# Attention loops written out, ordered first loads, and v projected in one run

## The reference, cut to what matters

```
h = layernorm(x)
q, k, v = split(h @ w_qkv + b_qkv)            # 16 heads of 16 features
attn = softmax(q @ k.T * 16**-0.5, axis=-1)   # per head, 4096 x 4096
x = x + layernorm((attn @ v) @ w_proj + b_proj)
x = x + layernorm(ffn(layernorm(x)))
```

## Time and profile before

| | before |
|---|---|
| median of 3 runs | 3265.24 us |
| profiled execution: time | 3264.68 us |
| profiled execution: span of the trace | 3262.9 us |
| mean granted TensorE clock | 0.967 |
| TensorE / DVE / ScalarE / GpSimd busy | 95 / 87 / 77 / 8% |

### The profile page before, as it was taken

The page is one execution under the profiler, slowest core; times in us unless marked ns, Lnnn a source line. Parts: engine busy times, 40 slices in busy tenths (PEclk is TensorE's granted clock), DMA queues, the critical chain, the costliest instruction groups (busy, mean ns, idle before and its releaser), DMA issues.

```text
span 3262.9 us, 80910 instructions
## 1 busy us (share of the span) xinstructions
PE 3107.3 (95%) x26983; PEld 1366.9 (42%) x26983; DVE 2833.9 (87%) x3108; ACT 2504.8 (77%) x4551; POOL 260.8 (8%) x810
## 2 busy tenths in 40 slices
PE   8799999999999999999999999999999999988883
PEld 3444443344344434443444344434434444456652
DVE  5389999999999999999999999999999999456666
ACT  6158888888888888888888888888888888733333
POOL 2300000000000000000000000000000000011103
PEclk9689999999999999999999999999999999989996
DMA  7700101010101011000101010101010100000001
GB/s 259 88 1 1 34 8 28 14 27 14 25 17 24 18 21 21 21 21 15 27 14 27 12 30 11 30 8 34 8 34 8 34 9 22 1 1 0 0 0 52
DMA packets 27390, 83.30 MB, mean 26 GB/s; under 512 B 4641, under 2 KB 15633, under 8 KB 24018
## 3 DMA queue, kind: packets, MB, share of 16 engines
q1 hardware_dynamic: 26818, 77.84, 10.7%
q0 software_dynamic: 272, 1.05, 0.1%
HBM read 57.90 MB, written 20.97 MB: 24 GB/s over the span
## 4 chain that ended last, share of the span: by engine, by line
PE 93%; DVE 2%; issue 2%; ACT 1%; DMA 1%; POOL 1%; DVEq 0%; SPq 0%; POOLq 0%; ACTq 0%
PE ps L1022 41%; PE ps L1031 36%; PE ps L1239 3%; PE ps L998 3%; PE ps L1188 2%; PE ps L957 2%; PE ps L1041 1%; PE ps L1228 1%; PE ps L971 1%; PE ps L1163 1%; PE ps L1049 1%; PE ps L949 1%; DMA q_stack<-qk_parts 1%; ACT q_raw L619 0%; PE ps L1205 0%
## 5 line engine op out<-in xcount | busy, mean ns | idle before, releaser
L750 DVE TENSOR_REDUCE partial<-ps 128x1 f32<-128x1024 f32 x2048 | 2482.1, 1223 | 179.1 <-PE ps L998 156.0
L569 ACT ACTIVATE work<-ps 128x512 f32<-128x512 f32 x4096 | 2203.3, 597 | 366.3 <-PE ps L1022 151.3
L998 PE MATMUL ps<-k_stack,q_stack 48*128 48x512 f32 x4096 | 1523.2, 451 | 25.2 <-DMA q_stack<-qk_parts 17.0
L1022 PE MATMUL ps<-q_stack,k_stack 64*128 64x512 f32 x4096 | 1513.1, 449 | 21.0 <-issue 19.4
L1031 PE MATMUL ps<-work,v_head 128*32 128x256 f32 x16384 | 1300.9, 392 | 0.0
L1022 PEld LDWEIGHTS ps<-q_stack,k_stack 64*128 64x128 f32 x4096 | 634.8, 185 | 822.2 <-ACT work L569 695.3
L998 PEld LDWEIGHTS ps<-k_stack,q_stack 48*128 48x128 f32 x4096 | 635.4, 187 | 60.9 <-DVE partial L750 32.8
L1031 PEld LDWEIGHTS ps<-work,v_head 128*32 128x32 f32 x16384 | 330.3, 108 | 701.3 <-ACT work L569 575.5
L415 POOL CAST nm_parts<-negmax 128x4 bf16<-128x4 f32 x128 | 24.8, 193 | 2267.5 <-DVE negmax L757 2266.6
L1239 PE MATMUL ps<-k_raw,q_raw 128*128 128x256 f32 x512 | 127.3, 405 | 17.8 <-ACT q_raw L619 17.8
L619 ACT ACTIVATE q_raw<-ps 128x1024 f32<-128x1024 f32 x32 | 32.7, 1023 | 131.5 <-PE ps L1228 131.5
(11 more groups left out here) (128 smaller groups left out, 1110.9 us busy)
## 6 DMA issues: line engine op xcount, KB each, us to landing
k_stack<-qk_parts SPq DMA_DIRECT2D x96, 256.0 KB, 4.2
q_stack<-qk_parts SPq DMA_DIRECT2D x96, 256.0 KB, 4.1
qk_parts<-qk_part SPq DMA_DIRECT2D x32, 512.0 KB, 2.8
x_sb<-L_attn_x SPq DMA_DIRECT2D x8, 512.0 KB, 10.9
out<-work SPq DMA_DIRECT2D x8, 512.0 KB, 2.9
k_raw<-L_ffn_aux_values SPq DMA_DIRECT2D x1, 1024.0 KB
work<-L_attn_w_qkv POOLq DMA_DIRECT2D x1, 768.0 KB, 7.7
q_raw<-L_ffn_aux_keys SPq DMA_DIRECT2D x1, 512.0 KB
```

Of the source, the lines that this page charges most:

```text
L569: act.activation(probs[:, g % DEPTH, a, :], ps[:, bank, :], ACT.Exp, scale=SCALE).then_inc(exp_done, 1)
L750: dve.tensor_reduce(partial[:, k // 4, k % 4:k % 4 + 1], ps[:, 2 * slot:2 * slot + 2, :], AX.XY, ALU.max).then_inc(max_used, 1)
L998: last = pe.matmul(ps[:, 2 * slot + e, :], q_stack[HALF:HALF + ROWS, b1, c * CH + (k // 4) * P:c * CH + (k // 4 + 1) * P], k_stack[HALF:HA ...
L1022: pe.matmul(ps[:, bank, :], k_stack[0:HALF, b, P * g:P * (g + 1)], q_stack[0:HALF, b, at:at + CH], start=True, stop=True).then_inc(s_ready, 1)
```

## The change

- TensorE's loop over two heads each is replaced by Python loops: heads 0 to 14 are written out.
- ScalarE's two nested loops are replaced by one Python loop over the passes 0 to 62, with constants in all waits.
- SP waits for groups 0 and 2 of parts_out, issues the six loads of head 0 for slots 3 to 5 (semaphore first_max_in), then the six for slots 0 to 2 (first_score_in), then waits for groups 1 and 3. The loads of head 1 wait for pv_done like those of all later heads.
- TensorE projects all eight chunks of v before the maximum pass, and none between its matmuls. The maximum pass waits for first_max_in, the first score for first_score_in.

```diff
@@ sync
-            for g in range(4):
-                sp.wait_ge(parts_out[g], 16 * (NC + 1))
-
-            def load_stack(h, b, after=None):
+            def load_first(slots, done):
+                for n in slots:
+                    for stack, qk, part in ((k_stack, 1, SLOT_K[n]), (q_stack, 0, SLOT_Q[n])):
+                        sp.dma_start(stack[SLOT_ROW[n]:SLOT_ROW[n] + D, 1, 0:T].bitcast(F32),
+                                     parts_dram[qk, part, 0:D, :]).then_inc(done, 16)
+
+            def load_stack(h, b, after):
                 for n, (row, pq, pk) in enumerate(zip(SLOT_ROW, SLOT_Q, SLOT_K)):
                     for m, (stack, qk, part) in enumerate(((k_stack, 1, pk), (q_stack, 0, pq))):
-                        if after is not None:
-                            sp.wait_ge(pv_done, after + (2 * n + m) * LOAD_EVERY)
+                        sp.wait_ge(pv_done, after + (2 * n + m) * LOAD_EVERY)
                         sp.dma_start(stack[row:row + D, b, 0:T].bitcast(F32), parts_dram[qk, part, h * D:(h + 1) * D, :]
                                      ).then_inc(stack_in[b], 16)
 
-            load_stack(0, 1)
-            load_stack(1, 0)
+            for g in (0, 2, 1, 3):
+                sp.wait_ge(parts_out[g], 16 * (NC + 1))
+                if g == 2:
+                    load_first((3, 4, 5), first_max_in)
+                    load_first((0, 1, 2), first_score_in)
+            load_stack(1, 0, 1 + CREDIT[pv_done])
@@ scalar
-            def attend_head(h, b):
-                with act.Fori(0, PAIRS - 1) as j:
-                    attend(h * PAIRS + j, (b, j * 2 + 2))
-                attend(h * PAIRS + (PAIRS - 1), (1 - b, 0))
-
-            with act.Fori(0, H // NB - 1) as r:
-                attend_head(r * NB, 1)
-                attend_head(r * NB + 1, 0)
-            attend_head(H - 2, 1)
-            with act.Fori(0, PAIRS - 1) as j:
-                attend(j + (H - 1) * PAIRS, (0, j * 2 + 2))
+            for it in range(ITS - 1):
+                h, j = (it + 1) // PAIRS, (it + 1) % PAIRS
+                attend(it, ((h + 1) % NB, 2 * j))
@@ tensor
-            with pe.Fori(0, NC // 4) as c2:
+            with pe.Fori(0, NC // 2) as c2:
                 for b in range(2):
                     for j in range(2):
                         project_v(c2 * 2 + b, b, j)
@@ tensor, maximum pass
-            pe.wait_ge(stack_in[1], 16 * LOADS)
+            pe.wait_ge(first_max_in, 16 * LOADS // 2)
             for c in range(AHEAD):
                 for k in range(16):
                     for e in range(2):
                         max_half(k, e, c, 1, c, k % 2)
-                    if k % 4 == 1:
-
-                        project_v(c * 2 + (NC // 2 + k // 8), k // 8, k // 4 % 2)
             pe.wait_ge(v_evac, 2 * NC + CREDIT[v_evac])
@@ tensor, attention
             pe.wait_ge(rows_set, 2)
+            pe.wait_ge(first_score_in, 16 * LOADS // 2)
             for g in range(LAG):
                 step(g, 0, 1, 0, chunks_ahead(1, 0), None)
-            with pe.Fori(0, H // NB - 1) as r:
-                next_loaded(r * NB, 1, r + 1)
-                next_loaded(r * NB + 1, 0, r + 2)
-            next_loaded(H - 2, 1, H // NB)
+            for h in range(H - 1):
+                next_loaded(h, (h + 1) % NB, h // NB + 1)
```

More of the change, by code:

```diff
@@ L208, in sandwich_kernel @@
         stack_in = [sem(f"stack_in{b}") for b in range(NB)]
+        first_max_in = sem("first_max_in")
+        first_score_in = sem("first_score_in")
         s_ready = sem("s_ready")
```

## The result

The changed kernel takes 3212.51 us (median of six runs, 3209.84 to 3213.14) against 3265.3 us before (six runs, 3263.46 to 3269.75): a ratio of 0.9834, 95% interval 0.9821 to 0.9847, or 53 us less. The forecast was 3199.1 us, 66 less, with a range of 3191 to 3215. The time lies near the upper end of that range, and outside the 3193 to 3207 to which the forecast gave a chance of 0.77.

A forecast was written before the change was run, and what follows sets the result against it. TensorE, busy 95% of the span, was taken as the bound, time being won where it stands still or another engine paces it. 3264.7 - 35.5 (loops) - 30.1 (start) = 3199.1 us, range 3191 to 3215.

The forecast's parts named there:

- Start: Ahead of attention: v in one run, ordered loads and a denser maximum pass win 30.1 us, bounds 28.8 to 34.0.
- the low end: Maximum pass: 28.8 us won if the whole pass runs at half clock, against 30.1 forecast.
- A second HAM failure mode: psum-queue depth-cycling: Maximum pass: small idle times between matmul groups bring the clock down; by this rule the gain is 28.8, not 30.1 us.
- Loops, the size: Attention passes 1 to 62: writing the loops out cuts 2571.34 us to 2535.8, a gain of 35.5 us.
- That is my price for every pass: Attention loop: every pass takes 40.90 us, as one pass of the already written-out heads does.
- a loss of 0.1 a pass: ScalarE in attention: bound on what constant waits could cost on each of 62 passes, 6 us; 0 was taken.
- Loops, the split: Attention loop: 29.8 us from six TensorE rounds at 5.0 and 5.7 us from about 30 ScalarE back edges.
- a start-up that gains only half: Rival, ahead of attention: second half of the v run at half clock, ending 16 us later; 3215 us, chance 0.06.
- The loops are not the cause: Rival, attention: the six passes have "issue" anyway, only the start-up wins, nothing of the 29.8; 3229 us, chance 0.04.
- the stop comes back in the straight code: Rival, attention: one in ten of about 200 code packets stops TensorE 1 us, returning 20 us; 3219 us, chance 0.06.
- slower: Rival, attention: all 200 code fetches late by over 0.33 us; at 0.5 us each 3299 us; chance 0.02.
- Instruction fetch mechanics: TensorE's attention loop: fetch is mostly hidden but a taken branch outside the window waits, so all 29.8 us goes.

The follow-up runs named there:

- the run of this part alone: Changed kernel with both engines' loops back, keeping only the ordered loads and v in one run: 3237.55 us, ratio 0.9904 to the kernel before.
- the run that waits for them: Changed kernel with v cut to four chunks first and eight pieces back between maximum matmuls, loads in the new order: 3224.49 us.
- with two waits and with one: Two: the changed kernel, 3212.51 us. One: the same without ScalarE's pv_done wait ahead of a step's first exponential, 3198.77 us.
- the half pieces: Changed kernel without ScalarE's pv_done wait, five v chunks before the maximum pass, the rest as half pieces within it: 3190.16 us.

## Why the prediction was right or wrong

*Start.* Right, in size and cause: 30.1 us forecast, 29.1 in the trace, 29.5 in the run of this part alone. v's end was put at 111.7 and is 111.2 (it began 1.2 us later, at full clock from the first piece: 1.00 from 83 to 98, where the kernel before had 0.89 from 82 to 98); six loads at about 100, 100.82 in the run that waits for them. GpSimd was done with the bias at 116.9 and not at 114, which nothing waited for. Of the 38 reductions I let 9 run at full clock; the 48.55 us from the first to the 39th (111.89 to 160.44) against 47.6 fit two or three, so the low end was nearer. That the first reduction came 0.7 us earlier than forecast made up for most of it. The rule that the prediction took from the Trainium skill ("TensorE: Matmul & The Clock Gate", A second HAM failure mode: psum-queue depth-cycling) points the same way, but the page speaks of a clock that swings between its two levels; here it fell once, between 115 and 117, and stayed at 0.50 to 170.

*Loops, the size.* 35.5 us forecast, 25.5 in the trace. The step that failed is "That is my price for every pass": 40.90 us, read between 2685.76 and 2726.66. That pass has TensorE written out but ScalarE inside its loop. The state after the change, both written out, stood one pass earlier in the same trace, between these two copies:

```profile
2644.67 0.39 ACT L592 ACTIVATE o_sb<-ps 128x256 f32<-128x256 f32 x1
...
2685.76 0.39 ACT L592 ACTIVATE o_sb<-ps 128x256 f32<-128x256 f32 x1
```

It is 41.09 us. The value products around a row step show why, in this pass and then in the one of 40.90: 1.50 and 1.44 us, the same two numbers as with two waits and with one.

```profile
2662.12 0.64 PE L1031 MATMUL ps<-work,v_head 128*32 128x256 f32 x8
...
2663.62 0.64 PE L1031 MATMUL ps<-work,v_head 128*32 128x256 f32 x8
```

```profile
2703.20 0.64 PE L1031 MATMUL ps<-work,v_head 128*32 128x256 f32 x8
...
2704.64 0.64 PE L1031 MATMUL ps<-work,v_head 128*32 128x256 f32 x8
```

62 passes at 0.16 us more are the 10.0 that are missing. I wrote that the trace doesn't show ScalarE's constant waits together with the maximum pass; it does, in this one pass. I gave a loss of 0.1 a pass as a bound, for want of a mechanism, and 0.16 is outside it; the runs name the mechanism: the late wait as an instruction of its own.

*Loops, the split.* Wrong: 29.8 us to TensorE's rounds and 5.7 to ScalarE's edges. Each alone is worth less than nothing (5 to 8 us more, by ratios and medians), both together 25.9. The sum came out near because the change made both edits, and that was luck: with TensorE's loop alone written out the same working would have missed by 37 us. The upper end of the range, which holds the measured time, was drawn for a start-up that gains only half; that didn't happen, and it covered an error elsewhere. The clue that I passed over is in the earlier trace rows and the waits of ScalarE in the kernel before: the longest wait of its exponentials was 3.5 us on TensorE, and a wait is put down to the engine that came last.

```profile
ACT work L569 <- PE ps L1022: 151.3, 217, 3.5
```

ScalarE's outer loop goes round at the same place as TensorE's, and I weighed only its inner loop, whose edge costs 0.2 us.

*"The loops are not the cause"*, *"the stop comes back in the straight code"*, *slower*: fell. No wait for "issue" is left ahead of a score; TensorE streams 9 packets of 16 KB in 120 us, as in the written-out head. The Trainium skill's rule on taken branches ("Runtime: NRT & Kernel Launch", Instruction fetch mechanics) agrees with these stops, if read for each engine by itself; I had applied it to TensorE alone.

*Tail.* 2.5 us more than before in the profiled run. Nothing ties it to the change: over the twelve profiled kernels the time behind the last output copy lies between 400.4 and 407.6 us, with the tail's code the same in all.

*What stays open.* Why the long passes differ so much among themselves: 45.3 to 46.4 us in the kernel before, 45.5 to 48.3 with both loops and the new start, 46.2 to 51.0 with one engine looping. The stops are nearly as long everywhere (19.0 to 20.1 us in six). What differs is the clock behind them: where a pass takes 45.3 us it is 0.79 in the first 8 us and then 1.00, where it takes 51.0 it is 0.71 and then 0.50 for 12 us more. What keeps it low wasn't tried. It also stays open how much of the gain of the half pieces comes from their size and how much from a start without a stop.

## What to carry to other kernels

Where several engines loop in step, look for the stop of each at the place where the loops go round, and take all of them away at once; with a wait put down to the engine that came last, a profile shows one and hides the other. When a price is read from a pass of the old kernel, check for every engine on the path that it already runs the code it will run after the change. When a loop is written out, look at where its waits go: the wait that is really late should be the one that rides on the instruction (here, first in the code), worth 13 us of 3212 for swapping two lines.

## What the runs showed of the hardware

An outer loop of ScalarE or TensorE whose body is a round of eight passes costs about 3.2 us (19.0 to 20.1 us in six) each time it goes round, an inner one of ScalarE, one pass long, 0.2 us (passes of 41.09 against 40.90). A separate semaphore wait ahead of an activation delays it by about 0.06 us when it is the late one (row steps of 1.50 against 1.44), and by nothing that the time shows when it is not (3199.66 against 3198.77 us). A short stop of TensorE costs more than itself: the 3.2 us became 4.4 to 10 us a round, as steps behind it ran at the lower clock, 2.16 us instead of 1.23. And in a pass that another engine paces, the clock was 1.00 with v halves between (102 to 131 us) and 0.50 to 0.53 without them; with whole pieces between, behind a stop of 3.41 us, it was 0.64.
